# Softplus in a state space scan: the rounding remainder made by ScalarE and GpSimd, the maximum left in PSUM

## The reference

```python
dt, Bm, Cm = jnp.split(ssm_p, [R, R + N], axis=-1)
dt = _rmsnorm(dt, dt_ln_w)
...
delta = jax.nn.softplus(dt @ Wdt.T + dt_bias)

def step(state, xs):
    d_t, B_t, C_t, u_t = xs
    dA = jnp.exp(d_t[..., None] * A)
    state = dA * state + (d_t * u_t)[..., None] * B_t[:, None, :]
    y_t = jnp.einsum('bdn,bn->bd', state, C_t)
    return (state, y_t)
```

## Time and profile before

| | |
|---|---|
| median of 3 runs | 4777.52 us (4775.16 to 4787.07) |
| profiled execution | 4765.77 us, span 4764.0 us |
| granted TensorE clock, mean | 0.958 |
| PE / DVE / ACT / POOL busy | 90% / 62% / 40% / 50% |
| scans, L1432 | 512, 1140.1 us, mean 2271 ns |
| multiplies, L511 | 512, 1197.4 us, mean some 2360 ns |
| idle before the multiplies, until a scan's end | 181.7 us |

### The profile page before, as it was taken

One profiled execution on the slowest core, in us unless ns is written; L12 is line 12 of the kernel. 1 busy time (PEld: TensorE's weight loads), 2 busy tenths in 40 slices (PEclk: granted clock), 3 DMA queues, 4 the chain that ended last, 5 costly groups with the idle time before them and its releaser, 6 DMA issues.

```text
span 4764.0 us, 66502 instructions
## 1 busy us (share of the span) xinstructions
PE 4282.5 (90%) x23408; PEld 2836.4 (60%) x23408; DVE 2971.8 (62%) x3131; ACT 1924.5 (40%) x2873; POOL 2381.3 (50%) x1017
## 2 busy tenths in 40 slices
PE   0886999989997999989997999989997999999998
PEld 0554777743465777744365777754365677753466
DVE  7995437479933546469933546469943446469943
ACT  1111224467721223467721223467731223367731
POOL 4443333378841333368851333368851333368852
PEclk9998999999997999999997999999998999999998
DMA  1113222310022222310021222310021222310021
GB/s 40 40 40 128 67 76 71 120 48 14 15 93 76 67 75 71 118 53 16 13 92 71 75 71 71 116 59 16 13 83 67 79 71 71 124 59 13 16 82 53
DMA packets 95278, 303.19 MB, mean 64 GB/s; under 512 B 11408, under 2 KB 15632, under 8 KB 92688
## 3 DMA queue, kind: packets, MB, share of 16 engines
q1 hardware_dynamic: 85776, 282.62, 18.0%
q10 hardware_dynamic: 9216, 16.78, 0.9%
HBM read 253.22 MB, written 46.14 MB: 63 GB/s over the span
## 4 chain that ended last, share of the span: by engine, by line
PE 59%; POOL 25%; issue 7%; DVE 6%; DMA 2%; ACT 1%; SPq 0%; DVEq 0%; POOLq 0%; ACTq 0%
PE psg L800 37%; POOL sb_wst L511 24%; PE psg L825 5%; PE psx L813 3%; PE psg L834 2%; PE psx L782 2%; PE psx L900 1%; PE psx L913 1%; PE psg L789 1%; PE psx L1011 1%; DVE sb_masks L1236 1%; PE psx L1099 1%; POOL sb_dg L463 1%; DVE sb_kfil L1230 1%; PE psx L890 1%
## 5 line engine op out<-in xcount | busy, mean ns | idle before, releaser
L477 POOL TENSOR_TENSOR sb_wl<-sb_raw,sb_wh 128x1024 fp32r<-128x1024 f32 x392 | 990.2, 2528 | 1939.0 <-ACT sb_wh L546 1939.0
L1432 DVE TENSOR_TENSOR_SCAN sb_wst<-sb_dA,psx 128x1024 f32<-128x1024 f32 x512 | 1140.1, 2271 | 52.4 <-ACT sb_dA L667 38.3
L546 ACT ACTIVATE sb_wh<-sb_raw 128x1024 fp32r<-128x1024 f32 x392 | 413.0, 1054 | 743.6 <-PE psg L800 335.1
L969 PEld LDWEIGHTS psx<-sb_dgB,sb_duT 64*128 64x128 f32 x4096 | 358.6, 189 | 542.8 <-DVE sb_wst L1432 333.1
L969 PE MATMUL psx<-sb_dgB,sb_duT 64*128 64x256 f32 x4096 | 590.0, 408 | 102.0 <-DVE sb_wst L1432 100.2
L667 ACT ACTIVATE sb_dA<-sb_dlt,sb_a_sb 128x504 f32<-128x504 f32 x1024 | 646.4, 705 | 59.4 <-DVE sb_wst L1432 49.1
L511 POOL TENSOR_TENSOR sb_wst<-sb_wst,sb_cb_lo 128x1024 f32<-128x1024 f32 x256 | 599.2, 2364 | 104.5 <-DVE sb_wst L1432 104.5
L511 POOL TENSOR_TENSOR sb_wst<-sb_wst,sb_cb_hi 128x1024 f32<-128x1024 f32 x256 | 598.2, 2358 | 77.2 <-DVE sb_wst L1432 77.2
L984 PE MATMUL psg<-sb_wst,sb_cst 64*64 64x512 f32 x4096 | 558.4, 618 | 10.9 <-POOL sb_wst L511 10.2
L800 PE MATMUL psg<-sb_xh,sb_wh 128*128 128x512 f32 x2112 | 548.6, 402 | 4.4 <-DVE sb_h L1558 4.4
L800 PE MATMUL psg<-sb_xh,sb_wl 128*128 128x512 f32 x2112 | 522.0, 389 | 0.0
(11 more groups left out here) (250 smaller groups left out, 5812.8 us busy)
## 6 DMA issues: line engine op xcount, KB each, us to landing
sb_raw<-in_w SPq DMA_DIRECT2D x360, 512.0 KB, 3.5
sb_h<-h_after_tok SPq DMA_DIRECT2D x8, 2048.0 KB, 7.8
sb_raw<-w_ffn_dequantized SPq DMA_DIRECT2D x32, 512.0 KB, 3.2
gates<-sb_gt ACTq DMA_DIRECT2D x64, 256.0 KB, 2.7
sb_gin<-gates SPq DMA_DIRECT2D x64, 256.0 KB, 2.6
h_after_tok<-sb_hT SPq DMA_DIRECT2D x4, 2048.0 KB, 14.6
h_after_tok<-sb_h SPq DMA_DIRECT2D x4, 2048.0 KB, 8.6
out<-sb_h SPq DMA_DIRECT2D x4, 2048.0 KB, 7.1
```

The lines of the kernel that those rows point to most:

```text
L477: pool.tensor_tensor(wl[:, i0 % SPL, :, :], raw[:, i0 % RAW, :, :], wh[:, i0 % SPL, :, :].bitcast(F32), ALU.subtract).then_inc(s_wl, 1)
L546: A(wh[:, i0 % SPL, :, :], raw[:, i0 % RAW, :, :], ACT.Copy).then_inc(s_wh, 1)
L969: ins_ = mm(psx[:, 2 * j + r, :].rearrange("p (a t e) -> p a t e", a=8, e=2)[:, :, :, e], duT[r0:r0 + 64, m % 2, i * P:(i + 1) * P], dgB[r ...
L1432: v.tensor_tensor_scan(wst[:, x, 4 * j:4 * j + 4, :, :].rearrange("p b n s -> p (b n s)"), dA[:, x, 4 * j:4 * j + 4, :, :].rearrange("p b ...
```

## The change

ScalarE's Relu now writes the maximum in place, into the PSUM tile, once Abs has read it. Exp stays in `spt` 0, w goes to `spt` 1, Ln to `dlt`, and a sixth pass makes 1 - w in `spt` 1. GpSimd gets an add of 128x512 a round, `rest_of_sum`: (1 - w) + e into `spt` 0. It stands ahead of the multiply of g = 2 of the round before. VectorE's `soft_sum` is one add instead of two operations, and waits for GpSimd's; it stands after scan g = 2 instead of g = 1. `drive_sum` adds the logarithm from `dlt`. In the gate stage GpSimd's splits of the last strips are written out so that the add for round 0 stands between two of them.

```diff
+                    def rest_of_sum(m):
+
+                        pool.wait_ge(s_sp3, b * DC + m + 1)
+                        pool.tensor_tensor(spt[:, 0, :], spt[:, 1, :], spt[:, 0, :], ALU.add).then_inc(s_rest, 1)
+
+                    split_loop(b, WIN0, 6)
+                    splits(b, GATE0 + 8, GATE0 + AHEAD + 8)
+                    rest_of_sum(0)
+                    splits(b, GATE0 + AHEAD + 8, WOUT0 + AHEAD)
-                    split_loop(b, WIN0, 8)
-                    splits(b, WOUT0, WOUT0 + AHEAD)
...
+                            if g == 2 and m < DC - 1:
+                                rest_of_sum(m + 1)
                             pool.wait_ge(s_scan, b * DC * G + m * G + g + 1 + CR_SCAN)
                             pool.tensor_tensor(x, x, cb, ALU.mult).then_inc(s_p, 1)
...
                         A(spt[:, 0, :], x, ACT.Abs, bias=dt_bias).then_inc(s_sp, 1)
-                        A(dlt[:, m % 2, :], x, ACT.Relu, bias=dt_bias).then_inc(s_sp, 1)
-                        act.wait_ge(s_sp, at + 2)
-                        A(x, spt[:, 0, :], ACT.Exp, scale=-1.0).then_inc(s_sp, 1)
+                        act.wait_ge(s_sp, at + 1)
+                        A(x, x, ACT.Relu, bias=dt_bias).then_inc(s_sp, 1)
+                        A(spt[:, 0, :], spt[:, 0, :], ACT.Exp, scale=-1.0).then_inc(s_sp, 1)
                         act.wait_ge(s_sp, at + 3)
-                        A(spt[:, 1, :], x, ACT.Identity, bias=C("one")).then_inc(s_sp1, 1)
+                        A(spt[:, 1, :], spt[:, 0, :], ACT.Identity, bias=C("one")).then_inc(s_sp1, 1)
                         act.wait_ge(s_sp1, b * DC + m + 1)
-                        A(spt[:, 0, :], spt[:, 1, :], ACT.Ln).then_inc(s_sp2, 1)
+                        A(dlt[:, m % 2, :], spt[:, 1, :], ACT.Ln).then_inc(s_sp2, 1)
+                        A(spt[:, 1, :], spt[:, 1, :], ACT.Identity, bias=C("one"), scale=-1.0).then_inc(s_sp3, 1)
...
-                        v.wait_ge(s_sp1, b * DC + m + 1)
-                        own.link(stt(x, spt[:, 1, :], 1.0, x, ALU.subtract, ALU.subtract))
-                        own.link(tt(x, dlt[:, m % 2, :], x, ALU.subtract))
+                        v.wait_ge(s_rest, b * DC + m + 1)
+                        own.link(tt(x, x, spt[:, 0, :], ALU.add))
...
-                        own.link(tt(x, spt[:, 0, :], x, ALU.add))
+                        own.link(tt(x, x, dlt[:, m % 2, :], ALU.add))
                         tt(du[:, :], x, u[:, m, :], ALU.mult).then_inc(s_dlt, 1)
...
-                            if g == 1 and m < DC - 1:
+                            if g == 2 and m < DC - 1:
                                 soft_sum(m + 1)
```

More of the change, by code:

```diff
@@ L308, in tower @@
         s_dA, s_w, s_scan, s_p, s_acc, s_y = sem("s_dA"), sem("s_w"), sem("s_scan"), sem("s_p"), sem("s_acc"), sem("s_y")
+        s_rest, s_sp3 = sem("s_rest"), sem("s_sp3")
         s_xsh, s_xsl = sem("s_xsh"), sem("s_xsl")
@@ L1401, in soft_sum @@
                         x = psg[:, 2, :]
-                        own = Own(v, s_own["sp"], b * 3 * DC + m * 3)
-                        v.wait_ge(s_sp1, b * DC + m + 1)
-                        own.link(stt(x, spt[:, 1, :], 1.0, x, ALU.subtract, ALU.subtract))
-                        own.link(tt(x, dlt[:, m % 2, :], x, ALU.subtract))
+                        own = Own(v, s_own["sp"], b * 2 * DC + m * 2)
+                        v.wait_ge(s_rest, b * DC + m + 1)
+                        own.link(tt(x, x, spt[:, 0, :], ALU.add))
                     def drive_sum(m):
                         x = psg[:, 2, :]
-                        own = Own(v, s_own["sp"], b * 3 * DC + m * 3 + 2)
+                        own = Own(v, s_own["sp"], b * 2 * DC + m * 2 + 1)
                         v.wait_ge(s_sp2, b * DC + m + 1)
```

## The result

The changed kernel takes 4829.5 us (median of four runs, 4820.4 to 4833.5), the kernel before beside it 4776.3: ratio 1.0105, 95% interval 1.0083 to 1.0128, so slower by some 53 us. The forecast was 4829, by +52. The profiled execution took 4830.6, span 4828.8; it had been forecast at 4817.7.

The account below looks back on a forecast made before the run. VectorE was taken as the bound, by a thin margin; with its wait for GpSimd's add, 4 x (14 x 0.90 + 0.38) = +51.9 us on 4777.5 gives 4829, range 4810 to 4862.

Parts of the forecast that it names:

- VectorE's wait behind GpSimd's queue: After scan g2, VectorE stands still 1.8 us a round for GpSimd's add, which stands behind g1's multiply.
- The round: One round of the scan stage gets 0.90 us longer, to 22.2; a stage's first round +0.38.
- The linked add to scan g3: On VectorE, soft_sum's one add, linked to its end, until scan g3 with one more wait: 0.80 us.
- ScalarE's cover: ScalarE's extra pass and Relu's wait add 0.85 us a round, hidden by 2.8 us before GpSimd can use the result.
- The gate stage: VectorE loses one add per block, GpSimd gets one between two splits; no time change, length kept to 1 us.
- Rival A: VectorE stays the bound and the removed add is a gain: 53 us less, 4725; chance 0.05.
- rival B: GpSimd's add is much cheaper (0.4) or its four multiplies start earlier: no difference, 4778; chance 0.06.
- Rival D: TensorE, standing still up to 2.5 us a round, loses a tenth of clock: +0.8 a round more, 4877; chance 0.03.
- carrying that over as a constant: The median of the runs, 11.7 us above the profiled execution before, was assumed to stay so for the changed kernel.

Follow-up runs that it names:

- sum_after_g3: The changed kernel with VectorE's soft_sum moved from behind scan g2 to behind scan g3, ahead of drive_sum; 4706.9 us, ratio 0.9843 to the kernel before.
- rest_before_g1: The changed kernel with GpSimd's add ahead of the multiply of g1 instead of g2; 4726.7 us, ratio 0.9878 to the kernel before.
- filled_gap: The changed kernel with one more f32 matmul of 128x512 a round where TensorE waits for scan g3; 4825.5 us, ratio 1.0075 to the kernel before.
- old_sum_after_g3: The kernel before with both operations of VectorE's soft_sum moved behind scan g3, ahead of drive_sum; 4754.6 us, ratio 0.9931 to the kernel before.

## Why the prediction was right, and where it was not

- **VectorE's wait behind GpSimd's queue.** Right, with its place and its releaser. Predicted 1.8 us a round, measured 1.61, since scan g2 ended at +11.31 and not at +11.17, after 0.15 of waiting for TensorE. GpSimd's add was put at 1.25, measured 1.26, spaced 1.22 to the next operation. Reckoned from scan g6's start (1147.84, one round of 22.22 ahead of 1170.06), GpSimd's add ends at +12.89 (predicted +12.91), VectorE's starts at +12.93 (+12.96), drive_sum at +15.95 (+15.95).
- **The round.** Predicted +0.90, measured 22.22 - 21.32 = +0.90; first round of block 0 with drive_sum at 1005.76 - 994.44 = 11.32 after the first scan, against 997.67 - 986.73 = 10.94: +0.38, as predicted.
- **The linked add to scan g3.** 0.80 predicted from the rows, 0.82 measured (1160.77 to 1161.59).
- **ScalarE's cover.** Right: 2.9 us (2.8 predicted). Relu from PSUM into PSUM takes 0.66.
- **The gate stage.** Right: no time. The first scan starts 108.67 us after TensorE's sums over the projection (994.44 - 885.77), and did so 108.68 after them before (986.73 - 878.05).
- **Rival A (the operation saved is a gain) and rival B.** Neither came, for the reason given: even the add of two columns leaves a wait. With the wait undone, the gain is 0.82 to 0.95 a round, near rival A's 0.88. But not all of it is the removed operation's: against the old pair of operations in the same place it is 0.72 behind g2 (21.22 - 20.50) and 0.44 behind g3 (20.81 - 20.37). The advice of "Perfetto Trace Analysis" in the Trainium skill ("Optimizing Scalar/DVE Operations"), that with VectorE saturated it may make sense to move some work even to GpSimd, holds in sum_after_g3 and rest_before_g1 and not in the changed kernel; the rows show what decides between them, the place in the other engine's queue. The same section of the Trainium skill adds that the two engines share an SBUF read port, so that moving work between them might not help; no such hindrance shows in the scans, whose longest duration stays 2289 ns.
- **Rival D was mis-sized, and the sum with it.** I gave TensorE's clock a chance of 0.03 and treated it as a loss of a tenth in every round, after a wait of up to 2.5 us; the wait is 1.78 in a steady round. The runs show a half in some rounds: +1.35 us in 9 of 60, and 1.4 more at the end of three of the stages. 9 x 1.36 + 3 x 1.44 is 16.6 us, less a hitch of 0.36 that each block of before has once: 15.1. The forecast's 51.9 and these are 67.0; the stages grew by 67.2. filled_gap has no long round, and 56.7 less the 6.1 of its stage ends is 50.6, which is 51.9 less before's hitches (50.5). The rounds' share is thus tied to TensorE's wait for scan g3, through filled_gap. The stage ends' 4.3 is not: the wait there is the same 2.54 before the change, and only the executions tell the two apart.
- **So the median's +53 meets the forecast's +52 partly by chance.** In the stages the mechanism gave 52, the clock 15 more, and outside them the executions differ by up to 25 us. The profiled execution of before was near the low end of these, which is why its time stood 12 under the median; carrying that over as a constant was an assumption that the second profiles don't bear out for the changed kernel (4830.6 and 4855.0 against medians of 4829.5 and 4841.4).

What stays open: which part of the stages' surplus the unprofiled runs had, since only profiled executions show it, and what decides behind which of equal waits the clock falls.

## What to carry to other kernels

Before work is moved from a full engine to one that is 14% idle, read what stands ahead of it in that engine's program at the moment when the result is wanted; the average idle share says nothing about that. Here one line decided between 1.05% slower and 1.6% faster: give the consumer's place as much distance as the producer's queue needs, or put the producer one item earlier. And set the old operations in the new place as a control: two of them moved, with nothing taken off VectorE, already gave 0.7% (old_sum_after_g3).

## What the runs showed of the hardware

- TensorE's granted clock fell to 0.50 (1.2 GHz) for some 3.7 us after waits of 2.40, 1.78 and 1.63 us in the changed kernel's rounds, but not after each such wait; with the wait for scan g3 cut to 0.73 by an added matmul (at most 1.36 in a block's first two rounds) it fell there in no round, though at the stage's end it still did. In the kernel before that wait was 1.09 in a steady round, and the clock fell only in the first round of a block, after 2.30 to 2.40. It did not fall after the 2.54 at the kernel before's stage ends, nor after the changed kernel's first 2.40 in a block. So the length of one wait doesn't decide it alone.
- All kernels start a scan stage at the low clock, after TensorE has waited 7.1 us: 0.50 in 989.10 to 991.00 of the kernel before, and in 996.80 to 999.00 of the changed one.
- One round in each block of the kernel before is 0.36 longer, at full clock; its cause wasn't looked for.
- A GpSimd add of two f32 inputs takes 1.26 us for 512 columns and 0.20 for 2 columns, a multiply of 1024 columns 2.36: a fixed part of about 0.2 and 2.1 ns a column.
- A dependent VectorE operation on the PSUM tile follows in 0.70 to 0.73 us, start to start. A scan behind such an operation follows in 0.97 where it waits for three semaphores more, and in 0.80 to 0.82 where it waits for one more. Two more waits ahead of an add left no trace: L1414 follows L1405 in 0.73 in old_sum_after_g3, as L1415, which has none, follows L1414.
